# Values of a windowed attention: 128-key products against pairs of 64-key products

## The chip, the cores and the metric

The kernel is one program on one core of a Trainium2 chip, written with explicit engine queues and semaphores. The metric is the device time of one launch in microseconds (us), the median of several runs. All data on the path looked at here are float32, and each float32 matmul leaves two records on TensorE (two weight loads and two passes).

## The reference

Two stacks follow each other over 16 sequences of 256 tokens with 128 features. First one causal attention with 16 heads of 8. Then six layers, each a windowed attention with 16 heads of 64 and a gated feed-forward part. The windowed attention is where the change lies:

```python
bk2, bv2 = (look(bk), look(bv))        # each window of 32 queries sees its own 32 keys and the 32 before
sim = jnp.einsum('bhwie,bhwje->bhwij', bq, bk2) * QK_SCALE
sim = jnp.where(mask, -jnp.finfo(sim.dtype).max, sim)
attn = jax.nn.softmax(sim, -1)
out = jnp.einsum('bhwij,bhwje->bhwie', attn, bv2)
...
x = attn_layer(shift_tokens(x), Wqkv[i], q_scale[i], k_scale[i], Wo[i]) + x
x = ffn_layer(shift_tokens(x), ln_g[i], ln_b[i], W1[i], b1[i], W2[i], b2[i]) + x
```

The last product, probabilities by values, is the one that is rearranged.

## The kernel before

All activations stay on the chip. The six layers run as a pipeline over sequences: `step(n, ...)` does the projections of sequence n (head), the scores and softmax of n-1 (mid) and the output and feed-forward part of n-2 (ffn), 96 sequence-layers in all. In the middle of a layer a hardware loop runs two steps a pass, six passes; the four steps around the change of layer are written out. Each engine has its own order of work, written out by hand in its `step`, and the engines are tied by counting semaphores: `need(engine, semaphore, value)` is a wait (L40), `need_apart` a wait followed by an increment of a semaphore of its own (L47).

A sequence has two tiles (t = 0, 1) of 128 tokens, and a tile four windows of 32. For a tile, `scores` (L1389) fills two PSUM banks, SC[:, 0] and SC[:, 1] (g = 0, 1), in which ScalarE's `put_mask` (L665) has put the mask before. VectorE takes the row maximum (`row_max` L901, `less_max` L906), ScalarE the exponential (`exps` L603), VectorE the sum (L913, L916), GpSimd divides (`normalise` L462), and VectorE turns 32x32 blocks (`turn` L923) into PTr. SyncE's `band` (L309, L311) then copies the blocks by DMA into BD, a banded matrix of 128 keys by 4 windows by 16 heads by 32 queries. Its other entries are zero, cleared once.

`values(n, t, g, par)` multiplies on TensorE, for each of eight heads, the 128 keys' values (128x64 weights) by 128 columns of BD (L1344). Even and odd heads go to partitions 0 to 63 and 64 to 127 of one bank. Of tile 1's first window, the keys of the window before lie in tile 0. They come as a second product (L1349) for four heads at once: `edge_values` gathers the last 32 rows of tile 0's values into Vx, and `band` (L315) the blocks into the block-diagonal BB. ScalarE's `o_evac` (L672) copies a bank to oT, and `output` (L1356) multiplies by Wo.

The same two banks SC serve scores and values in turn: `values` of tile 0 waits until VectorE has read tile 1's scores (s_sub), and the mask for the next sequence's tile 0 goes into a bank once `o_evac` has read tile 1's values from it. The order on TensorE around the change is:

- end of a step: `hidden` 0 and 1 (L1295, feed-forward, two PSUM banks in turn), `project_q` (L1302), `values(n-1, 0, 0)`, `hidden` 2, `values(n-1, 0, 1)`, `project_k` (L1302), `feed_out` (L1399);
- next step: `turn_x` (L1279), `turn_k` (L1370), `output` (L1356), `turn_k`, `project_q`, `turn_q` (L1379), `values(n-2, 1, 0)`, `turn_q`, `values(n-2, 1, 1)`, `scores(n-1, 0, 0)`, `output`, `scores(n-1, 0, 1)`.

`hidden` 2 reuses the bank of `hidden` 0 and waits for VectorE's `gated` 0 (L929), which waits for ScalarE's `gelus` (L609). `turn_k` waits for VectorE's `over_norms` (L987). ScalarE's order behind `values(n-2, 1, .)` is o_evac of bank 0, put_mask of bank 0, o_evac of bank 1, q_evac (L654), put_mask of bank 1.

Of the kernel before, what the change touches and what calls it, by code (L numbers as in the profile page):

```python
# [12 lines left out]
P = 128  # L13
# [3 lines left out]
TILES = SEQ // P  # L17
HA, DA = 16, 8
DEPTH, HEADS, DH = 6, 16, 64
# [30 lines left out]
def build(nc, x_in, wq_t, wk_t, wv_t, wo_t, wqkv, q_scale, k_scale, wo2, ln_g, ln_b, w1, b1, w2, b2,  # L50
          c_ident, c_winmask, c_causal, c_headmask, c_rot, out):
    with ExitStack() as ctx:
# [3 lines left out]
        def sem(name):  # L56
# [45 lines left out]
        BD = sb("BD", [P, TILES, NWIN, HEADS, WIN])  # L102
        BB = sb("BB", [P, 2, 4, 2, WIN])
        Vx = sb("Vx", [P, 2, 2, P])
# [37 lines left out]
        names = ("d_x d_x2 d_wa d_wap d_rot d_c d_wq d_wk d_wv d_qks d_wo d_ln d_ff d_out i_const i_zero i_pad i_dve i_pool i_sp i_guess i_bits d_id d_wav d_hm "  # L142
# [5 lines left out]
                 "s_tab s_ct s_nq s_nk d_bd0 d_bd1 d_vx")  # L148
        S = {n: sem(n) for n in names.split()}
        (d_x, d_x2, d_wa, d_wap, d_rot, d_c, d_wq, d_wk, d_wv, d_qks, d_wo, d_ln, d_ff, d_out, i_const, i_zero, i_pad, i_dve, i_pool, i_sp, i_guess, i_bits, d_id, d_wav, d_hm,  # L150
# [5 lines left out]
         s_tab, s_ct, s_nq, s_nk, d_bd0, d_bd1, d_vx) = [S[n] for n in names.split()]  # L156
# [13 lines left out]
        N_BAND = (2 * NWIN - 1, 2 * NWIN - 1 + 4)  # L170
        N_VX = 4
# [84 lines left out]
        def _(sp):  # L256
# [46 lines left out]
            def band(n, t):  # L303

                need_apart(sp, i_sp, s_T, 2 * n + t + 1)
                need_apart(sp, i_sp, s_o, 4 * n + 2 * t - 2)
                for w in range(NWIN):
                    rows = slice(32 * w, 32 * w + 32)
                    sp.dma_start(BD[rows, t, w, :, :], PTr[t][rows, 1, :, :]).then_inc(d_bd[t], 16)  # L309
                    if w:  # L310
                        sp.dma_start(BD[32 * w - 32:32 * w, t, w, :, :], PTr[t][rows, 0, :, :]).then_inc(d_bd[t], 16)  # L311
                if t:
                    edge = PTr[t][0:WIN, 0, :, :].rearrange("p (g c k) i -> p g c (k i)", g=2, c=4)
                    for c in range(4):
                        sp.dma_start(BB[32 * c:32 * c + 32, :, c, :, :].rearrange("p g k i -> p g (k i)"),  # L315
                                     edge[:, :, c, :]).then_inc(d_bd[t], 16)

            def edge_values(n, par):

                need_apart(sp, i_sp, s_ve, 2 * n + 1)  # L320
                need_apart(sp, i_sp, s_o, 4 * n - 4)
                last = V[par][P - WIN:P, 0, :].rearrange("p (g c n) -> p g c n", g=2, c=4)
# [1226 lines left out]
```

## Time and profile before

| | |
|---|---|
| median of 3 runs | 3595.3 us (3594.93 to 3595.39) |
| profiled execution, span | 3598.4 us |
| TensorE busy | 3482.8 us, 97% |
| VectorE busy | 3160.0 us, 88% |
| ScalarE busy | 3061.0 us, 85% |
| GpSimd busy | 2352.0 us, 65% |
| chain that ended last | TensorE 62%, ScalarE 19%, issue 10%, VectorE 5% |

The span is from the first to the last instruction of one execution under the profiler, and is what that execution took. The runs without a profile lie 3 us lower. Busy time counts an engine's own instructions. A pass on TensorE is recorded with a latency that overlaps the next passes, so its pace is read from starts, or from the chain, and not from the length of one record.

### The profile page before, as it was taken

What the parts mean: (1) busy time and instruction counts of PE and PEld (TensorE: products, weight loads), DVE (VectorE), ACT (ScalarE), POOL (GpSimd) and SP (SyncE); (2) the same over time, 40 slices, a digit from 0 to 9 for tenths busy, and PEclk for the clock granted to TensorE, in tenths of its full rate; (3) what the DMA queues carried; (4) which work ended last, traced back from release to release, by engine and by line L of the source; (5) the groups of instructions that cost most, each with busy time, mean ns of one, the idle gap of its engine ahead of it and who ended that gap; (6) DMA issues with size and microseconds to landing.
All of it is one profiled execution on the core that took longest, in us unless ns stands there. A gap on an engine that the chain in (4) does not pass through costs nothing.

```text
span 3598.4 us, 95666 instructions
## 1 busy us (share of the span) xinstructions
PE 3482.8 (97%) x33868; PEld 2390.4 (66%) x33868; DVE 3160.0 (88%) x5848; ACT 3061.0 (85%) x5121; POOL 2352.0 (65%) x1607
## 2 busy tenths in 40 slices
PE   8999899999999999999999999999999999999998
PEld 6777466666666666666666666666666666666666
DVE  6998889888988988888888898888889888888986
ACT  5766688888888888888888888888888888888886
POOL 2001677777777777777777677777777777777774
PEclk9999999999999999999999999999999999999999
DMA  2000011112211112211112111112111112211112
GB/s 63 0 0 0 21 34 39 38 33 54 52 34 34 39 36 52 50 40 33 34 40 53 46 39 38 32 36 58 47 33 39 38 33 55 52 33 34 39 37 54
DMA packets 182965, 136.67 MB, mean 38 GB/s; under 512 B 97612, under 2 KB 135632, under 8 KB 182800
## 3 DMA queue, kind: packets, MB, share of 16 engines
q1 hardware_dynamic: 180019, 125.00, 14.8%
q10 hardware_dynamic: 2781, 9.51, 0.9%
q8 instruction: 98, 1.61, 0.2%
q14 instruction: 67, 0.55, 0.1%
HBM read 19.04 MB, written 2.10 MB: 6 GB/s over the span
## 4 chain that ended last, share of the span: by engine, by line
PE 62%; ACT 19%; issue 10%; DVE 5%; SPq 1%; POOL 1%; DMA 1%; ACTq 0%; DVEq 0%; POOLq 0%
PE ps L1302 12%; PE ps L1389 10%; PE ps L1356 10%; PE ps L1344 7%; PE ps L1379 4%; PE ps L1370 4%; PE ps L1160 3%; ACT L750 3%; ACT area L603 2%; DVE area L987 2%; ACT G L609 2%; ACT L609 2%; ACT area L618 2%; ACT area L625 2%; PE ps L1295 2%
## 5 line engine op out<-in xcount | busy, mean ns | idle before, releaser
L1302 PE MATMUL ps<-Wqkv,xsT 128*128 128x512 f32 x2304 | 1112.5, 605 | 8.7 <-ACT area L638 3.8
L449 POOL TENSOR_TENSOR area<-area,tab 128x512 f32<-128x512 f32 x768 | 970.0, 1273 | 146.7 <-ACT area L618 146.1
L1302 PEld LDWEIGHTS ps<-Wqkv,xsT 128*128 128x128 f32 x2304 | 391.2, 189 | 351.4 <-issue 295.0
L462 POOL TENSOR_TENSOR area<-area,lsum 128x1024 f32<-128x1024 f32 x192 | 365.5, 1904 | 383.2 <-DVE lsum L916 383.2
L456 POOL TENSOR_TENSOR AQb<-AQb,area 128x1024 f32<-128x1024 f32 x192 | 455.2, 2371 | 15.1
L456 POOL TENSOR_TENSOR area<-area 128x1024 f32<-128x1024 f32 x192 | 455.0, 2370 | 9.0 <-DVE area L976 1.5
L618 ACT ACTIVATE area<-ps 128x1024 f32<-128x1024 f32 x384 | 393.6, 1025 | 66.2 <-PE ps L1302 55.1
L1389 PEld LDWEIGHTS ps<-kbd,area 128*32 128x32 f32 x12288 | 313.2, 109 | 196.1 <-issue 113.4
L1344 PE MATMUL ps<-BD,area 128*64 128x128 f32 x6144 | 421.5, 279 | 17.7 <-issue 11.3
L1344 PEld LDWEIGHTS ps<-BD,area 128*64 128x64 f32 x6144 | 329.4, 137 | 158.8 <-issue 100.2
L1389 PE MATMUL ps<-kbd,area 128*32 128x128 f32 x12288 | 415.6, 276 | 17.0 <-ACT kbd L648 5.7
L625 ACT ACTIVATE area<-area 128x1024 f32<-128x1024 f32 x384 | 405.1, 1055 | 3.2
L1356 PE MATMUL ps<-Wo,area 128*128 128x128 f32 x3072 | 385.2, 279 | 1.2 <-ACT area L672 0.7
L1356 PEld LDWEIGHTS ps<-Wo,area 128*128 128x128 f32 x3072 | 357.6, 192 | 20.7 <-issue 19.6
L654 ACT ACTIVATE area<-ps 128x512 f32<-128x512 f32 x384 | 217.9, 593 | 132.6 <-PE ps L1379 132.6
L901 DVE TENSOR_REDUCE mx<-ps 128x8 f32<-128x512 f32 x384 | 263.2, 686 | 49.7 <-PE ps L1389 49.7
L923 DVE STREAM_TRANSPOSE area<-area 128x1024 f32<-128x1024 f32 x192 | 239.2, 1246 | 61.7 <-POOL area L462 61.2
L1295 PE MATMUL ps<-xnT,W 128*128 128x256 f32 (+1 forms) x1152 | 288.3, 386 | 1.8 <-ACT xnT L684 1.5
L672 ACT ACTIVATE area<-ps 128x512 f32<-128x512 f32 x384 | 227.0, 591 | 71.0 <-PE ps L1349 66.8
L906 DVE TENSOR_TENSOR area<-ps,mx 128x512 f32<-128x512 f32 x384 | 264.8, 690 | 9.9
L1295 PEld LDWEIGHTS ps<-xnT,W 128*128 128x128 f32 (+1 forms) x1152 | 197.8, 178 | 91.3 <-issue 63.6
L941 DVE TENSOR_REDUCE ss<-area 128x16 f32<-128x1024 f32 x192 | 233.6, 1216 | 22.4 <-ACT area L625 21.2
(136 smaller groups left out, 6630.6 us busy)
## 6 DMA issues: line engine op xcount, KB each, us to landing
BD<-area SPq DMA_DIRECT2D x1344, 64.0 KB, 2.0
Vx<-area SPq DMA_DIRECT2D x384, 32.0 KB, 1.9
Wqkv<-ffn_Wqkv ACTq DMA_DIRECT2D x18, 512.0 KB, 4.0
BB<-area SPq DMA_DIRECT2D x384, 16.0 KB, 1.8
x2s<-x2s SPq DMA_DIRECT2D x96, 56.0 KB, 2.0
Wo<-ffn_Wo SPq DMA_DIRECT2D x6, 512.0 KB, 4.3
W<-ffn_W SPq DMA_DIRECT2D x6, 341.0 KB
x2s<-x2s SPq DMA_DIRECT2D x96, 0.2 KB, 1.7
```

The source lines that it names most:

```text
L449: pool.tensor_tensor(b4[:, :, here], q4[:, :, there], s4[:, :, here], ALU.mult).then_inc((s_bq, s_bk)[j], 1)
L456: pool.tensor_tensor(AQ[t][:, col], AQ[t][:, col], BQ[:, col], ALU.add).then_inc(s_rot, 1)
L462: pool.tensor_tensor(p3, p3, lsum[:, 1, :].unsqueeze(2).broadcast_to([P, HEADS, 2 * WIN]), ALU.mult).then_inc(s_pn, 1)
L618: act.activation(QH[:, j * INNER:(j + 1) * INNER], PJ[:, :], ACT.Copy).then_inc((s_hq, s_hk)[j], 1)
L625: act.activation(SQ[:, col], QH[:, col], ACT.Square).then_inc((s_sqq, s_sqk)[j], 1)
L901: dve.tensor_reduce(mx[:, 8 * g:8 * g + 8], s3[:, g, :, :], AX.X, ALU.max).then_inc(s_mx, 1)
L906: dve.tensor_tensor(Pr[:, t, 512 * g:512 * g + 512].rearrange("p (h k) -> p h k", k=2 * WIN), s3[:, g, :, :], mx[:, 8 * g:8 * g + 8].unsqu ...
L1295: last = mm(TR[c % 2][0:m, half * SEQ:(half + 1) * SEQ], W1[:, half * FF + f0:half * FF + f0 + m], xnT[:, :], start=True, stop=True)
L1302: last = mm(PJ[:, b * 512:(b + 1) * 512], xsT[:, par, t * P:(t + 1) * P], Wqkv[:, w0:w0 + 512], start=True, stop=True)
L1344: last = mm(slot[DH * k:DH * k + DH, c * P:(c + 1) * P], V[par][:, t, h * DH:(h + 1) * DH], BD[:, t, :, h, :], start=(c == 0), stop=False, ...
L1356: last = mm(EXO[:, t * P:(t + 1) * P], oT[:, t, c, :], Wo[:, c, :], start=(c == 0), stop=(c == PAIRS - 1))
L1389: last = mm(SC[32 * w:32 * w + 32, g, (c % 4) * P:(c % 4 + 1) * P], qT[:, c, 32 * w:32 * w + 32], kbd[:, c, :, k0:k0 + 2 * WIN], start=Fal ...
```

## The change

The 128 keys of a tile are taken as two halves r of 64. Each half multiplies only its own 64 queries (two windows, 64 columns), uses its own 64 rows of the array and writes its own PSUM bank: bank r now holds the queries of half r for all 16 heads, where bank g held all queries for eight heads. For a head there are two products of 64 keys by 64 value columns by 64 queries instead of one of 128 by 64 by 128. BD shrinks to half.

What crosses a half is done afterwards as products over 32 rows. The keys of window 1 for the queries of window 2 are 16 products in either tile. Tile 0's last 32 keys for tile 1's first window are 16 more in tile 1. Their blocks are in the new BE. Vx, BB and `edge_values` (eight DMAs a sequence) go away, and one DMA into BE is added. `values` does a whole tile in one call, with one increment of s_o, and stands once where it stood twice: for tile 1 before the second `turn_q`, for tile 0 after `hidden` 2. Its three waits are `need_apart`.

```diff
-        BD = sb("BD", [P, TILES, NWIN, HEADS, WIN])
-        BB = sb("BB", [P, 2, 4, 2, WIN])
-        Vx = sb("Vx", [P, 2, 2, P])
+        BD = sb("BD", [P, TILES, 2, HEADS, WIN])
+        BE = sb("BE", [P, TILES, HEADS, WIN])
...
-        N_BAND = (2 * NWIN - 1, 2 * NWIN - 1 + 4)
-        N_VX = 4
+        N_BAND = (2 * NWIN - 1, 2 * NWIN)
...
                 need_apart(sp, i_sp, s_T, 2 * n + t + 1)
-                need_apart(sp, i_sp, s_o, 4 * n + 2 * t - 2)
+                need_apart(sp, i_sp, s_o, 2 * n + t - 1)
+                rows = [slice(32 * w, 32 * w + 32) for w in range(NWIN)]
                 for w in range(NWIN):
-                    rows = slice(32 * w, 32 * w + 32)
-                    sp.dma_start(BD[rows, t, w, :, :], PTr[t][rows, 1, :, :]).then_inc(d_bd[t], 16)
-                    if w:
-                        sp.dma_start(BD[32 * w - 32:32 * w, t, w, :, :], PTr[t][rows, 0, :, :]).then_inc(d_bd[t], 16)
-                if t:
-                    edge = PTr[t][0:WIN, 0, :, :].rearrange("p (g c k) i -> p g c (k i)", g=2, c=4)
-                    for c in range(4):
-                        sp.dma_start(BB[32 * c:32 * c + 32, :, c, :, :].rearrange("p g k i -> p g (k i)"),
-                                     edge[:, :, c, :]).then_inc(d_bd[t], 16)
-
-            def edge_values(n, par):
-
-                need_apart(sp, i_sp, s_ve, 2 * n + 1)
-                need_apart(sp, i_sp, s_o, 4 * n - 4)
-                last = V[par][P - WIN:P, 0, :].rearrange("p (g c n) -> p g c n", g=2, c=4)
-                for c in range(4):
-                    sp.dma_start(Vx[32 * c:32 * c + 32, par, :, :], last[:, :, c, :]).then_inc(d_vx, 16)
+                    sp.dma_start(BD[rows[w], t, w % 2, :, :], PTr[t][rows[w], 1, :, :]).then_inc(d_bd[t], 16)
+                    if w % 2:
+                        sp.dma_start(BD[rows[w - 1], t, 1, :, :], PTr[t][rows[w], 0, :, :]).then_inc(d_bd[t], 16)
+                    elif w or t:
+                        sp.dma_start(BE[rows[w - 1], t, :, :], PTr[t][rows[w], 0, :, :]).then_inc(d_bd[t], 16)
 
             def shift(n, last):
...
-                    edge_values(n - 1, 1 - par)
...
-            pool.memset(BB[:, :, :, :, :], 0.0).then_inc(i_zero, 1)
...
-                need(act, s_o, 4 * n - 4)
+                need(act, s_o, 2 * n - 2)
...
             def o_evac(n, t, g):
-                need(act, s_o, 4 * n + 2 * t + g + 1)
+                need(act, s_o, 2 * n + t + 1)
                 if t == 0 and g == 0:
                     need(act, s_wo, n)
-                act.activation(oT[:, t, 4 * g:4 * g + 4, :], SC[:, g, :].rearrange("p (c n) -> p c n", c=4),
+                half = slice(2 * WIN * g, 2 * WIN * (g + 1))
+                act.activation(oT[:, t, :, half], SC[:, g, :].rearrange("p (c n) -> p c n", c=PAIRS),
                                ACT.Copy).then_inc(s_oe, 1)
...
-            def values(n, t, g, par):
-
-                T = 2 * n + t
-                if g == 0:
-                    need(pe, s_ve, T + 1)
+            def values(n, t, par):
+
+                need_apart(pe, i_pe, s_ve, 2 * n + t + 1)
+                need_apart(pe, i_pe, d_bd[t], 16 * N_BAND[t] * (n + 1))
+                if t:
+                    need_apart(pe, i_pe, s_oe, 4 * n + 2)
+                else:
+                    need_apart(pe, i_pe, s_sub, 4 * n + 4)
+                for c in range(PAIRS):
+                    for r in range(2):
+                        keys = slice(2 * WIN * r, 2 * WIN * (r + 1))
+                        for k in range(2):
+                            h = 2 * c + k
+                            mm(SC[DH * k:DH * k + DH, r, 2 * WIN * c:2 * WIN * (c + 1)], V[par][keys, t, h * DH:(h + 1) * DH],
+                               BD[keys, t, :, h, :], start=(c == 0), stop=False, skip_group_check=True)
+                for c in range(PAIRS):
+                    for k in range(2):
+                        h = 2 * c + k
+                        last = mm(SC[DH * k:DH * k + DH, 1, 2 * WIN * c:2 * WIN * c + WIN], V[par][WIN:2 * WIN, t, h * DH:(h + 1) * DH],
+                                  BE[WIN:2 * WIN, t, h, :], start=False, stop=True, skip_group_check=True)
                     if t:
-                        need(pe, d_vx, 16 * N_VX * (n + 1))
-                    need(pe, d_bd[t], 16 * N_BAND[t] * (n + 1))
-                if t:
-                    need(pe, s_oe, 4 * n + g + 1)
-                else:
-                    need(pe, s_sub, 4 * n + 3 + g)
-                slot = SC[:, g, :]
-                for c in range(4):
-                    for k in range(2):
-                        h = 2 * (4 * g + c) + k
-                        last = mm(slot[DH * k:DH * k + DH, c * P:(c + 1) * P], V[par][:, t, h * DH:(h + 1) * DH],
-                                  BD[:, t, :, h, :], start=(c == 0), stop=False, skip_group_check=True)
-                if t:
-                    for k in range(2):
-                        half = slice(DH * k, DH * k + DH)
-                        last = mm(slot[half, :].rearrange("p (c n) -> p c n", c=4)[:, :, 0:WIN], Vx[:, par, g, half],
-                                  BB[:, g, :, k, :], start=False, stop=True, skip_group_check=True)
+                        for k in range(2):
+                            h = 2 * c + k
+                            last = mm(SC[DH * k:DH * k + DH, 0, 2 * WIN * c:2 * WIN * c + WIN], V[par][P - WIN:P, 0, h * DH:(h + 1) * DH],
+                                      BE[P - WIN:P, t, h, :], start=False, stop=True, skip_group_check=True)
                 last.then_inc(s_o, 1)
...
                 if ffn:
-                    values(n - 2, 1, 0, par)
+                    values(n - 2, 1, par)
                 if mid:
                     turn_q(n - 1, 0, 1)
-                if ffn:
-                    values(n - 2, 1, 1, par)
                 if mid:
                     scores(n - 1, 0, 0)
                 if ffn:
@@ -1477,12 +1463,10 @@
                     hidden(n - 2, 1)
                 if head:
                     project_q(n, 1, par)
-                if mid:
-                    values(n - 1, 0, 0, 1 - par)
                 if ffn:
                     hidden(n - 2, 2)
                 if mid:
-                    values(n - 1, 0, 1, 1 - par)
+                    values(n - 1, 0, 1 - par)
                 if head:
                     project_k(n, 1, par)
                 if ffn:
```

## Rows read from the trace of the kernel before

**Rows 1.** The page, section 1: busy us (share of the span), instructions of each engine.

```profile
PE 3482.8 (97%) x33868; PEld 2390.4 (66%) x33868; DVE 3160.0 (88%) x5848; ACT 3061.0 (85%) x5121; POOL 2352.0 (65%) x1607
```

**Rows 2.** Windows, two loop steps: length, busy us (instructions) of each engine, granted clock, DMA.

```profile
2178.00:2244.10 66.10, 64.76 (x634) 44.20 (x632) 59.11 (x107) 58.57 (x93) 47.66 (x33) 1.00 0.16 36
```

**Rows 3.** TensorE in order of time, one loop step: start, length in us, group [idle before].

```profile
2207.90 1.09 PE L1344 MATMUL ps<-BD,area 128*64 128x128 f32 x16
...
2208.93 1.10 PE L1295 MATMUL ps<-xnT,W 128*85 128x256 f32 x4
...
2210.97 1.98 PE L1302 MATMUL ps<-Wqkv,xsT 128*128 128x512 f32 x4
...
2214.13 0.38 PE L1279 MATMUL ps<-ident,xst 128*128 128x128 f32 x2
...
2214.69 0.66 PE L1370 MATMUL ps<-ident,area 128*128 128x128 f32 x4 [0.17 <-DVE area L987]
...
2219.68 1.09 PE L1344 MATMUL ps<-BD,area 128*64 128x128 f32 x16
...
2220.61 0.39 PE L1349 MATMUL ps<-BB,Vx 128*64 128x128 f32 x4
...
2222.76 1.08 PE L1389 MATMUL ps<-kbd,area 128*32 128x128 f32 x32
```

**Rows 4.** VectorE and ScalarE in order of time, the same step.

```profile
2193.83 0.69 DVE L901 TENSOR_REDUCE mx<-ps 128x8 f32<-128x512 f32 x1 [0.47 <-PE ps L1389]
...
2208.16 0.47 DVE L929 SCALAR_TENSOR_TENSOR H<-ps,b1s,G 128x256 f32<-128x256 f32 x1
...
2213.41 1.22 DVE L987 TENSOR_TENSOR area<-area,ps 128x1024 f32<-128x1024 f32 x1
...
2221.05 0.60 ACT L672 ACTIVATE area<-ps 128x512 f32<-128x512 f32 x1
...
2221.68 0.60 ACT L665 ACTIVATE ps<-wmask_f 128x512 f32<-128x512 f32 x1
```

**Rows 5.** Chain in order of time: start, us, line, passes.

```profile
2217.60 1.72 PE ps L1302 x4
...
2219.32 0.44 PE ps L1379 x4
...
2221.59 1.02 PE ps L1344 x16
...
2222.83 1.01 PE ps L1389 x32
```

**Rows 6.** TensorE in windows of 0.03 and 0.05 us: passes that run in them.

```profile
2222.76 0.32 PE L1389 MATMUL ps<-kbd,area 128*32 128x128 f32 x4
...
215.27 0.38 PE L1149 MATMUL ps<-area,AqT 32*128 32x128 f32 x2
```

**Rows 7.** Groups of weight loads by form: busy us, mean ns, idle before.

```profile
L1344 PEld LDWEIGHTS ps<-BD,area 128*64 128x64 f32 x6144 | 329.4, 137 | 158.8 <-issue 100.2 <-DMA BD<-area 56.7 <-DMA BB<-area 2.0
...
L1389 PEld LDWEIGHTS ps<-kbd,area 128*32 128x32 f32 x12288 | 313.2, 109 | 196.1 <-issue 113.4 <-ACT kbd L648 69.0 <-ACT ps L665 2.3
```

**Rows 8.** Waiting and register operations of the queues (L40), 2222.2 to 2223.2.

```profile
L40 PEldq ALU_OP  x2: 32/32/32, 2222.3 to 2223.0; - x2
```

**Rows 9.** GpSimd's increment (L47) between 2207 and 2210, and GpSimd in order of time.

```profile
L47 POOLq EVENT_SEMAPHORE  x1: 17/17/17, 2208.4 to 2208.4; - x1
...
2207.24 1.91 POOL L462 TENSOR_TENSOR area<-area,lsum 128x1024 f32<-128x1024 f32 x1 [1.09 <-DVE lsum L916]
```

**Rows 10.** DMA issues: SyncE's queue in order of time; the page, section 6.

```profile
2215.09 2.56 SPq L315 DMA_DIRECT2D BB<-area  x4
...
BB<-area SPq DMA_DIRECT2D x384, 16.0 KB, 1.8
```

**Rows 11.** DMA queue of instructions, 1915 to 2113 and 2113 to 2434: packets, MB, share.

```profile
q8 instruction: 13, 0.21, 0.5%
...
q8 instruction: 1, 0.02, 0.0%
```

More of the change, by code:

```diff
@@ L139, in build @@
         nmx = sb("nmx", [P, 2, HA])
-        names = ("d_x d_x2 d_wa d_wap d_rot d_c d_wq d_wk d_wv d_qks d_wo d_ln d_ff d_out i_const i_zero i_pad i_dve i_pool i_sp i_guess i_bits d_id d_wav d_hm "
+        names = ("d_x d_x2 d_wa d_wap d_rot d_c d_wq d_wk d_wv d_qks d_wo d_ln d_ff d_out i_const i_zero i_pad i_dve i_pool i_sp i_guess i_bits i_pe d_id d_wav d_hm "
                  "a_lnc a_lnr a_lnn a_xh a_xt a_xe a_qk a_qe a_ke a_km a_v a_ve a_s a_mx a_e a_t a_te "
@@ L147, in build @@
                  "s_o s_oe s_ve s_wo s_r1 d_sh s_lnc s_lnr s_lnn s_ln s_xn s_xne s_h s_gl s_g s_y s_xc "
-                 "s_tab s_ct s_nq s_nk d_bd0 d_bd1 d_vx")
+                 "s_tab s_ct s_nq s_nk d_bd0 d_bd1")
         S = {n: sem(n) for n in names.split()}
-        (d_x, d_x2, d_wa, d_wap, d_rot, d_c, d_wq, d_wk, d_wv, d_qks, d_wo, d_ln, d_ff, d_out, i_const, i_zero, i_pad, i_dve, i_pool, i_sp, i_guess, i_bits, d_id, d_wav, d_hm,
+        (d_x, d_x2, d_wa, d_wap, d_rot, d_c, d_wq, d_wk, d_wv, d_qks, d_wo, d_ln, d_ff, d_out, i_const, i_zero, i_pad, i_dve, i_pool, i_sp, i_guess, i_bits, i_pe, d_id, d_wav, d_hm,
          a_lnc, a_lnr, a_lnn, a_xh, a_xt, a_xe, a_qk, a_qe, a_ke, a_km, a_v, a_ve, a_s, a_mx, a_e, a_t, a_te,
@@ L155, in build @@
          s_o, s_oe, s_ve, s_wo, s_r1, d_sh, s_lnc, s_lnr, s_lnn, s_ln, s_xn, s_xne, s_h, s_gl, s_g, s_y, s_xc,
-         s_tab, s_ct, s_nq, s_nk, d_bd0, d_bd1, d_vx) = [S[n] for n in names.split()]
+         s_tab, s_ct, s_nq, s_nk, d_bd0, d_bd1) = [S[n] for n in names.split()]
         PJ = ps[:, 0:2, :].rearrange("p a b -> p (a b)")
@@ L373, in _ @@
             pool.memset(x2s[:, :, :, :], 0.0).then_inc(i_zero, 1)
-            pool.memset(BB[:, :, :, :, :], 0.0).then_inc(i_zero, 1)
             pool.wait_ge(d_hm, 16)
-            pool.wait_ge(i_zero, 5)
+            pool.wait_ge(i_zero, 4)
             pool.wait_ge(i_pad, 2)
@@ L589, in _ @@
             attention_steps(act, a_step)
-            act.wait_ge(i_zero, 7)
+            act.wait_ge(i_zero, 6)
             def x_evac(n, par):
```

## The prediction, made before the kernel was run

> **What bounds the kernel now.** I read the page's first section, then the windows, then one step in order of time, engine by engine, and last the chain. TensorE is busy for 97% of the span [rows 1], and at full clock in the middle of a layer: of the 66.10 us of one pass of the loop (two steps) it is busy for 64.76, VectorE for 59.11, ScalarE for 58.57 [rows 2]. So a step lasts 33.05 us, and whatever lengthens or shortens TensorE's own sequence moves the end, unless TensorE then only waits. The 97% hides how near some waits are: in the order of time TensorE's value groups (L1344, L1349) fill stretches in which the other engines are just getting ready [rows 3, 4]. These decide the case.
>
> How fast the small products go: a pass is one of the two records that each float32 matmul leaves. Four passes over 512 columns take 1.72 us, 0.43 each; four over 128 columns take 0.44, 0.11 each; so a pass costs its moving columns at 0.84 ns [rows 5]. The 16 value passes take 1.02 us and the 32 score passes 1.01 [rows 5]: 128 columns each, two and four side by side, eight groups of 0.11 plus 0.15 for changing shape. The 256-column group of L1295 says the same: 4 x 0.216 = 0.86, and 1.02 from its start to the next [rows 3]. Passes of different column tiles start together (four L1389 in a window of 0.03 us), and so do two that use different 32-row tiles (L1149) [rows 6]. Weight loads are recorded with 109 ns for 32 columns and 137 for 64 [rows 7]: 0.88 ns a column, so some 56 ns for 64 columns apart from a fixed delay that overlaps.
>
> **The change, part by part**, in one loop step.
>
> *Main products.* 32 passes of 128 columns for each tile t become 64 passes of 64 columns, four side by side. 64 columns stream in 0.054 us, their 64 weights load in 0.056: I take 0.057 for each group of four, 16 groups, 0.91 us. Before: 16 pairs at 0.11, 1.75 us.
>
> *Crossing blocks.* Tile 0 had none; tile 1 had eight passes, 0.44 us. Now tile 0 has 32 passes and tile 1 has 64, each with 32 moving but still 64 weight columns. By streaming a group would cost 0.027, by its weights 0.056; a weight load can hide only behind a pass as long as itself, so I take 0.057, and both tiles need 16 groups (pairs for tile 0, fours for tile 1): 0.91 us. With two changes of shape (128 to 64 rows, then 32 rows), 0.30, a block lasts 2.12 us. The lower bound (0.028) is 1.66 us.
>
> *Tile 0's place.* Before, half of its values (2207.90) stood between project_q and hidden(2) (2208.93) [rows 3]. Without it hidden(2) reaches TensorE at once, but needs VectorE's gated(0), which ends at 2208.16 + 0.47 = 2208.63; it would start at 2208.70 (L1370 started 0.06 after its L987). VectorE is no help: from the row maximum at 2193.83, which itself waited for TensorE, to gated(0) it has 27 rows with three pauses, 0.5 us in all [rows 4]. So TensorE stands idle for 0.9 us that was filled. Then hidden(2) 1.02, block 2.12: project_k at 2211.84 instead of 2210.97, +0.87. Later turn_k waits for L987 (ends 2214.63): TensorE could have been there at 2214.13 + 0.22 = 2214.35 but started at 2214.69 [rows 3, 4]; 0.34 of the delay vanishes in this wait. Net +0.53.
>
> *Tile 1's place.* Before: values, crossing, turn_q, values, crossing, 2219.68 to 2222.76, 3.08 us [rows 3]. Behind the first half ScalarE read bank 0 (L672 at 2221.05) and wrote the mask there (L665, ends 2222.28) while TensorE did the other half [rows 4]; the scores of bank 0 need that mask. In the new order both banks finish together, and only turn_q (0.59) covers the two. The first half's last product began at 2220.72, the mask was usable at 2222.28 + 0.06: 1.62 us. The new block's last product begins 1.97 after 2219.68, at 2221.65, so the scores start at 2223.27 instead of 2222.76: +0.51. ScalarE's next work (second bank, q_evac, mask of bank 1) is queued behind its wait, but the scores of bank 0 (1.01) and the output products behind them cover it.
>
> *Issue.* Tile 1's block is 256 instructions in 1.97 us, tile 0's 192. The queue's own records show how fast they can be sent: between two register operations of TensorE's sequencer, at 2222.3 and 2223.0, lie the 64 instructions of one score group, 11 ns each [rows 8]. 256 would need 2.8 us; those sent ahead during the transposes come off. From none ahead (+0.85) to all ahead (0) I take +0.15, since the sequencer no longer waits there for the last band transfer. That makes tile 1 +0.66.
>
> *TensorE's own increments* (three per block): on GpSimd such an increment ran at 2208.4, in the middle of L462 (2207.24 to 2209.15) and ahead of L456, which stands before it in GpSimd's order [rows 9], so it does not drain an engine; I take nothing. If it drained TensorE, blocks would lose what was sent ahead: up to +1.
>
> *Transfers.* Four BB and four Vx transfers go, one BE comes. BB's were the last to land for tile 1: issued 2215.09 to 2217.65, 1.8 us to landing [rows 10], 0.2 us before the values at 2219.68. That wait was hidden; its margin grows to some 2 us, worth nothing by itself. ScalarE's reads have new strides and the same size: nothing. GpSimd clears less memory in the first part, off the chain.
>
> Sum: 0.53 + 0.66 = 1.19 us a step, 96 steps, 114 us; on the profiled span 3598.4 + 114 = 3712, and on the median of the runs, which is 3.1 us under that span, 3709.
>
> The Trainium skill (TensorE: Matmul & The Clock Gate, "Wait — 56ns, not 53.3ns?") says that starts of matmuls are never closer than about 25 ns. By that rule the 128 passes of tile 1 would need 3.2 us and the 96 of tile 0 2.4, about 1.8 us a step more than my sum, and the kernel would take near 3880. By that rule, the trace disagrees: it has four starts inside 0.03 us [rows 6].
>
> **Rivals.**
> *Row halves in turn.* Passes in the same columns but different rows do not overlap once 64-wide. For it: no row shows four tiles in both directions. Against it: L1149. Main groups then cost 0.11 and tile 1's crossing too: +0.9 for tile 0, +1.8 for tile 1, 3.9 us a step, 3970.
> *An issue limit.* The fastest pace of the chain is 32 passes in 1.01 us, 0.0315 each [rows 5]. If that were sending and not streaming, 128 passes would take 4.0 us and 96 take 3.0: +3.2 us, 4.4 a step, 4020. Against it: the 11 ns above.
> *The loop's code no longer stays in place.* In a layer's unrolled steps and first loop pass instruction transfers run (13 in 198 us); in the other five passes one in 321 us [rows 11]. A pass has 634 matmul and 633 weight-load records, plus some 50 others [rows 2]; 608 are added, 45% more. If that is too long, each jump back waits for a transfer: 0.5% of 16 engines over 198 us for 13 is 1.2 us each, and about 2 to land, as the band's; partly covered by queued passes. 30 jumps at 1 to 3 us: +30 to +90 on top of my sum, 3740 to 3800.
> The Trainium skill (Runtime: NRT & Kernel Launch, "Instruction fetch mechanics") gives TensorE 2048 instructions in blocks of 256 and a stall for a jump out of them; the new pass has near 1,930, so close that its position among the blocks would decide. That the present loop is not fetched again agrees with the rows.
> *Crossing passes that cost only their issue* (the other side). If weights of 32-row tiles load while other rows' tiles run, they shrink towards 7 ns, and the block to 1.3 us. Tile 0: 2211.02, lost in the wait of L1370; tile 1: scores at 2222.55, -0.2. 3575. It decides once a block is under 1.6 us, below my bound by streaming; L1344 and L1389 show no pass below its columns.
> *Streaming bound only* (0.028): blocks of 1.66 us, +0.07 and +0.05 to +0.3, 3605 to 3630.
>
> **Numbers.** Forecast 0.62 (own range 3670 to 3765), loop code 0.14, row halves 0.07, issue limit 0.05, streaming bound 0.06, issue-only crossings 0.06. A difference of 0.2% (7 us) is what can be told from none. Faster 0.06, same 0.03, slower 0.91. The range 3620 to 3870 leaves out row halves, the issue limit, issue-only crossings and a little of streaming, some 0.19 in all.
>
> **What would show it.** After: L1344's groups of 64 in about 1 us with four starts together; the crossing lines in about 0.9 us each; TensorE idle near 0.9 us before L1295's 85-column group, released by VectorE's H; idle near 0.9 us before the scores, released by ScalarE's L665 mask; less wait at L1370 for L987. It is wrong if blocks are not near 2.1 us (weights or issue), if either wait is missing, or if instruction transfers go on through the loop.

## The result and the profile after

The changed kernel takes 3775.2 us (median of 4 runs, 3774.2 to 3782.0) against 3595.4 (3594.9 to 3596.6) in the same session: 1.050 times as long, 95% interval 1.0487 to 1.0517. The forecast was 3709. It names the right sign and, as will be seen, some two thirds of the loss (114 of 180 us); the rest is what the rival on the loop's code describes. The measured time lies above the forecast's own range (3670 to 3765), inside that rival's (3740 to 3800) and inside the wide range (3620 to 3870). Each group of runs below was taken beside runs of the kernel before, whose median lay between 3595 and 3598 from group to group, so a few us between groups mean nothing. One of the ten executions of e2_before_no_loop took 4921.3 us at a granted clock of 0.655 and is left out of its ratio.

The page of the changed kernel: busy us and instructions of each engine, from section 1, and the queue of instructions from section 3 (packets, MB, share of 16 engines).

```profile
span 3772.4 us, 124129 instructions
...
PE 3480.3 (92%) x48460; PEld 2424.7 (64%) x48460; DVE 3176.6 (84%) x5848; ACT 3057.5 (81%) x5121; POOL 2346.6 (62%) x1606
...
q8 instruction: 427, 7.00, 0.8%
```

TensorE has 14,592 more passes than in [rows 1], and yet is busy for 2.5 us less; its share fell from 97% to 92%. So the span's 174 us are idle time of TensorE. The waits name it. Before, TensorE's longest ones were (line that waits, what released it, us in total, times, longest):

```profile
PE ps L1370 <- ACT area L654: 33.4, 96, 1.2
PE ps L1370 <- DVE area L987: 15.2, 72, 1.4
PE ps L1344 <- issue: 11.3, 11, 2.3
```

After, in the same view (L1377 are the scores, L1281 `hidden`, L1265 `turn_x`, L1358 `turn_k`, L1344 `output`):

```profile
PE ps L1377 <- ACT ps L650: 79.3, 96, 1.9
PE ps L1281 <- DVE H L915: 69.3, 96, 2.2
PE ps L1265 <- issue: 43.8, 30, 2.2
PE ps L1358 <- ACT area L639: 33.2, 96, 1.0
...
PE ps L1344 <- issue: 6.7, 6, 1.3
```

Three new waits: the scores for ScalarE's mask and hidden 2 for VectorE's H, both 96 times, and `turn_x` for nothing that the profile shows, 30 times. The wait for VectorE's norms (old L987) is nearly gone (2.3 us, twice). 79.3 + 69.3 + 43.8 - 15.2 is 177 us, the 174 within what smaller waits add and take. The queue of instructions from 2113 to 2434 us, where [rows 11] have a single packet:

```profile
q8 instruction: 40, 0.66, 0.9%
```

So instruction transfers now go on through the loop, which the prediction had named as a sign of being wrong. One step in order of time on TensorE, after (L1288 projections, L1327 main products, L1332 crossing, L1387 `feed_out`, L1367 `turn_q`):

```profile
2229.41 1.09 PE L1281 MATMUL ps<-xnT,W 128*85 128x256 f32 x4 [0.71 <-DVE H L915]
2230.43 1.16 PE L1327 MATMUL ps<-BD,area 64*64 64x64 f32 x64
2231.52 1.12 PE L1332 MATMUL ps<-BE,area 32*64 32x32 f32 x32
2232.57 1.98 PE L1288 MATMUL ps<-Wqkv,xsT 128*128 128x512 f32 x4
2234.39 1.50 PE L1387 MATMUL ps<-W,H 128*128 128x128 f32 x12
2237.41 0.43 PE L1265 MATMUL ps<-ident,xst 128*128 128x128 f32 x2 [1.52 <-issue]
2237.68 0.60 PE L1358 MATMUL ps<-ident,area 128*128 128x128 f32 x4
...
2242.59 1.16 PE L1327 MATMUL ps<-BD,area 64*64 64x64 f32 x64
...
2244.74 0.66 PE L1367 MATMUL ps<-ident,area 128*128 128x128 f32 x4
...
2246.24 1.08 PE L1377 MATMUL ps<-kbd,area 128*32 128x128 f32 x32 [0.84 <-ACT ps L650]
```

Read from start to start: the main products of tile 0 take 1.09 us and its crossing 1.05, the block 2.14; tile 1's block 2.15, with 256 instructions. The row of L1265 is the surprise: `feed_out` ends near 2235.9, and `turn_x`, which was to follow at once as in [rows 3], comes 1.5 us later. It stands at the head of a loop pass. Steps from one `turn_x` to the next that hold no such stall last 34.08 us at least and often 34.17 (before: 33.05); those that end in one last 35.3 to 36.8, one of them 37.7.

### The profile page after: what moved, and what is told of

Its sections match the earlier page's. It is cut to its first block, busy times and chain, and to the rows that moved or that the text cites. A ratio compares the mean times of both kernels' runs of the same rounds, so it can differ in the third digit from the quotient of the medians.

```text
span 3772.4 us, 124129 instructions
## 1 busy us (share of the span) xinstructions
PE 3480.3 (92%) x48460; PEld 2424.7 (64%) x48460; DVE 3176.6 (84%) x5848; ACT 3057.5 (81%) x5121; POOL 2346.6 (62%) x1606
## 4 chain that ended last, share of the span: by engine, by line
PE 66%; DVE 11%; ACT 11%; issue 8%; DMA 2%; SPq 1%; POOL 1%; DVEq 0%; ACTq 0%; POOLq 0%
PE ps L1288 13%; PE ps L1344 10%; PE ps L1377 9%; PE ps L1327 6%; PE ps L1332 5%; PE ps L1387 3%; PE ps L1358 3%; PE ps L1281 3%; DVE ss L927 3%; PE ps L1146 3%; DVE lsum L899 3%; ACT area L610 3%; DVE area L962 2%; PE ps L1367 2%; DMA x2s<-x2s 2%
## 5 line engine op out<-in xcount | busy, mean ns | idle before, releaser
L1288 PE MATMUL ps<-Wqkv,xsT 128*128 128x512 f32 x2304 | 1112.6, 605 | 9.0 <-ACT area L623 3.8
L1288 PEld LDWEIGHTS ps<-Wqkv,xsT 128*128 128x128 f32 x2304 | 391.3, 189 | 339.3 <-issue 278.8
L1377 PE MATMUL ps<-kbd,area 128*32 128x128 f32 x12288 | 419.6, 277 | 97.4 <-ACT ps L650 79.3
L1377 PEld LDWEIGHTS ps<-kbd,area 128*32 128x32 f32 x12288 | 316.4, 110 | 284.6 <-issue 178.1
L1344 PE MATMUL ps<-Wo,area 128*128 128x128 f32 x3072 | 394.7, 282 | 8.1 <-issue 6.7
L1344 PEld LDWEIGHTS ps<-Wo,area 128*128 128x128 f32 x3072 | 361.5, 193 | 35.8 <-issue 27.9
L1281 PE MATMUL ps<-xnT,W 128*128 128x256 f32 (+1 forms) x1152 | 287.0, 385 | 70.8 <-DVE H L915 69.3
L1281 PEld LDWEIGHTS ps<-xnT,W 128*128 128x128 f32 (+1 forms) x1152 | 197.0, 178 | 221.6 <-DVE H L915 147.9
L962 DVE TENSOR_TENSOR area<-area,ps 128x1024 f32<-128x1024 f32 x192 | 228.7, 1191 | 76.4 <-PE ps L1367 75.6
L650 ACT ACTIVATE ps<-wmask_f 128x512 f32<-128x512 f32 x384 | 229.3, 597 | 64.0 <-DVE area L892 60.9
L420 POOL COPY xres<-x2s 128x256 f32 (+1 forms) x80 | 31.8, 397 | 383.7 <-DVE x2s L987 383.7
```

Source lines behind the costliest of these rows:

```text
L962: dve.tensor_tensor(AQ[t][:, col].rearrange("p (h d) -> p h d", d=DH), QH[:, col].rearrange("p (h d) -> p h d", d=DH), cosp[:, t, j, :].un ...
L1281: last = mm(TR[c % 2][0:m, half * SEQ:(half + 1) * SEQ], W1[:, half * FF + f0:half * FF + f0 + m], xnT[:, :], start=True, stop=True)
L1288: last = mm(PJ[:, b * 512:(b + 1) * 512], xsT[:, par, t * P:(t + 1) * P], Wqkv[:, w0:w0 + 512], start=True, stop=True)
L1344: last = mm(EXO[:, t * P:(t + 1) * P], oT[:, t, c, :], Wo[:, c, :], start=(c == 0), stop=(c == PAIRS - 1))
L1377: last = mm(SC[32 * w:32 * w + 32, g, (c % 4) * P:(c % 4 + 1) * P], qT[:, c, 32 * w:32 * w + 32], kbd[:, c, :, k0:k0 + 2 * WIN], start=Fal ...
```

## The experiments

Twelve kernels. The first four ask where the time at the head of the loop comes from, the next two what a crossing product costs, the last six what the two waits are worth. A ratio is against the kernel before, with its 95% interval. Where TensorE's steps are "written out", its twelve middle steps of a layer stand in the program one after the other, without the hardware loop; the other engines keep their loops.

**e1_no_loop: the change, TensorE's steps written out.**

```diff
-            stack_steps(pe, step)
+            stack_steps(pe, step, looped=False)
```

> The changed kernel with TensorE's program written out in full (no hardware loop on TensorE; the other engines keep theirs, the order of work is the same). Theory: the waits and the longer order cost about 1.1 us a step (a step without a jump lasts 34.1 us instead of 33.05), and the rest of the +180 us is a stall of TensorE at the jump back, since a pass of the loop no longer stays in its instruction memory. Then this kernel takes 3775 - 70 = 3705 us (3695 to 3715), every step lasts about 34.1 us, and the instruction transfers stay near 400. Rival: what costs is the transfer of the code itself, or the sending of more instructions, everywhere: then the time stays at 3765 to 3780.

Measured 3713.5 us, 1.0319 (1.0301 to 1.0336). Waits of TensorE, written out:

```profile
PE ps L1381 <- ACT ps L654: 74.0, 96, 1.9
PE ps L1285 <- DVE H L919: 69.6, 96, 2.2
PE ps L1362 <- ACT area L643: 39.8, 96, 1.1
```

`turn_x` no longer waits; the mask and H waits stand as they were. Nearly as many instruction packets come as in the changed kernel (364 against 427), and nearly all of them are hidden here (ten waits inside the crossing products, 5.4 us together, are not): 62 us go with the jumps, 2.1 for each of 30. Without them the kernel takes close to what was forecast for it (3709).

**e2_before_no_loop: the kernel before, written out the same way.** 

> The kernel before with TensorE's program written out in full. Theory of the jumps: the loop of before fits, so it pays no stall and there is nothing to gain but what registers cost; the written-out steps of before last 32.8 to 33.0 us against 33.05 in the loop, so 3575 to 3596 us, although instruction transfers rise from 98 to about 270. Rival (transfers themselves cost TensorE time): 170 more transfers make it slower, by 0.4 us each at the rate of the changed kernel (70 us for its 330 more... some 0.2 each), 3625 to 3660.

Measured 3604.0, 1.0017 (1.0007 to 1.0027), inside neither range: writing out gives nothing back, nor does it cost 30 us. TensorE waits 18.4 us at the values (26 times) for nothing that the profile shows, where before had 11.3 (11 times); only one of the 26 has an instruction packet shortly ahead of it, so this is not shown to be late code. So the 62 us are the changed kernel's own. Set like against like, both written out, the change costs 3713.5 - 3604.0 = 109.5 us, and the other 70 of the 180 come only with the loop.

**e7_no_crossing: the change without its crossing products,** in the loop. What crosses a half is left out of the output. A pass of the loop loses 384 instructions, of some 1,930.

```diff
-                               BD[keys, t, :, h, :], start=(c == 0), stop=False, skip_group_check=True)
-                for c in range(PAIRS):
...
+                               BD[keys, t, :, h, :], start=(c == 0), stop=True, skip_group_check=True)
```

> The changed kernel without its crossing products (L1332, L1337), so their part of the output is left out. A pass of TensorE's loop then has some 1,550 instructions instead of 1,930 (before: 1,310). Theory: it fits again, so instruction transfers fall from 427 to near 110, and no pass of the loop has the idle 1.5 us before turn_x; with 1.1 us less in each block the time is 3520 to 3560 us. Rival (it is not the length but any growth of the loop): transfers stay above 300 and every second step is longer by over 1 us: 3590 to 3630.

Measured 3533.7 (one run). Nearly every step in the loop lasts 32.55 to 32.65 us and TensorE is never idle ahead of `turn_x` there. Its queue of instructions:

```profile
q8 instruction: 115, 1.88, 0.2%
```

With about 1,550 instructions in a pass (1,930 less 384) the stall is absent; but this kernel also does less work, so the next one changes the length alone.

**e12_before_four_steps: the kernel before, four steps in a pass** (three passes a layer, some 2,630 instructions each), same order and work.

```diff
-                with eng.Fori(0, SEQS // 2 - 2) as k:
-                    for odd in range(2):
-                        step(eng.snap(base + 2 * k + (2 + odd)), 2 * k + (2 + odd), odd, True, True, True, layer)
+                with eng.Fori(0, (SEQS - 4) // each) as k:
+                    for i in range(each):
+                        step(eng.snap(base + each * k + (2 + i)), each * k + (2 + i), i % 2, True, True, True, layer)
```

> The kernel before with four steps to a pass of TensorE's loop instead of two (three passes a layer instead of six); the work and its order are the same. Its pass has some 2,620 instructions. Theory (length alone makes the stall): it no longer fits, instruction transfers rise from 98 to about 250, and each of the 12 jumps back costs 1.5 to 2.5 us: 3595 + 18 to 30 = 3613 to 3625 us. Rival (the stall needs the dense blocks of the changed kernel): 3590 to 3602.

Measured 3650.3, 1.0152 (1.0139 to 1.0166), 53 us over the kernel before in the same session: the direction expected, about twice the size. Its waits:

```profile
PE ps L1279 <- issue: 22.6, 12, 2.3
PE ps L1344 <- DMA BD<-area: 10.8, 19, 1.1
...
PE ps L1344 <- issue: 9.6, 8, 2.3
...
PE ps L1356 <- issue: 6.5, 4, 2.1
```

Two jumps back in each of six layers, 12 in all, and 12 stalls of 1.9 us ahead of `turn_x` (old L1279), where before's list of waits has none. So the length of a pass makes the stall, in the kernel before too. The stalls are 22.6 of 53 us. Four more just behind a jump (L1356, 6.5 us) follow an instruction packet in the same way (see e11 for that reading). Most of the rest is a longer wait for the band (10.8 us against 1.8) and 9.7 us more of busy TensorE; the eight waits at the values (L1344, 9.6 us) follow no packet and were there before.

**e4_half_weights and e8_eight_columns: what bounds a crossing product.** e4 takes 32 of a head's 64 value columns in the crossing products, e8 takes 8 of their 32 moving columns; the other half, and the other three quarters, of the crossing output are left out. For e4 (the products into bank 0 likewise)

```diff
-                        last = mm(SC[DH * k:DH * k + DH, 1, 2 * WIN * c:2 * WIN * c + WIN], V[par][WIN:2 * WIN, t, h * DH:(h + 1) * DH],
+                        last = mm(SC[DH * k:DH * k + WIN, 1, 2 * WIN * c:2 * WIN * c + WIN], V[par][WIN:2 * WIN, t, h * DH:h * DH + WIN],
```

and for e8

```diff
-                        last = mm(SC[DH * k:DH * k + DH, 1, 2 * WIN * c:2 * WIN * c + WIN], V[par][WIN:2 * WIN, t, h * DH:(h + 1) * DH],
-                                  BE[WIN:2 * WIN, t, h, :], start=False, stop=True, skip_group_check=True)
+                        last = mm(SC[DH * k:DH * k + DH, 1, 2 * WIN * c:2 * WIN * c + 8], V[par][WIN:2 * WIN, t, h * DH:(h + 1) * DH],
+                                  BE[WIN:2 * WIN, t, h, 0:8], start=False, stop=True, skip_group_check=True)
```

> The changed kernel with the crossing products (L1332, L1337) on only the first 32 of the 64 value columns of each head, so half of their output is left out; their number and their 32 moving columns stay. Theory: a group of crossing passes is bound by loading 64 weight columns (0.057 us); with 32 it takes 0.03, so tile 0's crossing falls from 1.05 us to about 0.6 and the block from 2.14 to 1.7 us. Rival: each pass is bound by its sending or by a fixed floor: the crossing stays at 1.05 us.

> The changed kernel with 8 moving columns instead of 32 in each crossing product, so three quarters of the crossing output are left out; weights as they were. Theory (bound by 64 weight columns): tile 0's crossing stays at 1.05 us and the time at 3765 to 3780. Rival (bound by streaming): it falls to 0.4 us or less and the time to under 3700.

Measured 3726.8 and 3772.3 (one run each; the changed kernel 3775.2). TensorE in order of time at tile 0, e4:

```profile
2242.95 1.16 PE L1327 MATMUL ps<-BD,area 64*64 64x64 f32 x64
2244.04 0.69 PE L1332 MATMUL ps<-BE,area 32*32 32x32 f32 x32
2244.67 1.98 PE L1288 MATMUL ps<-Wqkv,xsT 128*128 128x512 f32 x4
```

The same place, e8:

```profile
2232.44 1.16 PE L1327 MATMUL ps<-BD,area 64*64 64x64 f32 x64
2233.53 1.10 PE L1332 MATMUL ps<-BE,area 32*64 32x8 f32 x32
2234.56 0.70 PE L1288 MATMUL ps<-Wqkv,xsT 128*128 128x512 f32 x1
```

Half the weight columns: 1.05 us become 0.63. A quarter of the moving columns: 1.03, no change. Each of the 16 groups of a tile's crossing products costs what 64 weight columns cost, 0.06 us, though it streams only 32. Whether that is the load itself or something else that goes with the 64 columns, such as the 64 output rows, these two runs do not separate.

**e10_split_no_loop: the H wait filled again.** Tile 0's main products (part 0 of `values`) go back ahead of hidden 2, its crossing (part 1) stays behind; written out, so to be set against e1.

```diff
                     project_q(n, 1, par)
+                if mid:
+                    values(n - 1, 0, 1 - par, 0)
                 if ffn:
                     hidden(n - 2, 2)
                 if mid:
-                    values(n - 1, 0, 1 - par)
+                    values(n - 1, 0, 1 - par, 1)
```

> e5's split of tile 0's block with TensorE's program written out, so without jumps. Theory: the wait for VectorE's H costs 0.35 us a step net of one change of shape and of the slack before turn_k: 3713 - 34 = 3679 us (3670 to 3690). Rival (the split has no gain, what e5 gained was noise of the jumps): 3705 to 3715.

Measured 3668.5, 1.0195 (1.0179 to 1.0211), 45 us under e1 and 11 under the 3679 expected. The H wait (69.6) is gone; it is worth 45 and not 70, because 26.8 us come back as a wait of L1332, here the main products, for the band's transfers, in 32 of 96 steps. It has the lowest median of the changed versions that compute everything (e9's runs overlap it) and is still 71 us slower than the kernel before in the same session.

**e5_split_tile0: the same in the loop.** 

> The changed kernel with tile 0's block cut in two: the main products ahead of hidden 2, the crossing products behind it. e3 showed that the whole block ahead only moves the wait (TensorE then stood before turn_k for over_norms, because hidden 2 and the third gelu came 1.2 us later). Theory: as in the kernel before, about 1.1 us ahead of hidden 2 covers the wait for VectorE's H without making hidden 2 late; against the changed kernel project_k comes 0.65 us earlier (0.8 of wait less 0.15 for one more change of shape), 0.3 of it is lost before turn_k: -0.35 us a step, 3740 us (3725 to 3755), with the idle time before the 85-column L1281 and before turn_k both under 15 us. Rival: any order but the one of before loses the same: 3765 to 3830.

Measured 3763.6, 1.0464 (1.0446 to 1.0483): only 12 us under the changed kernel and 24 over what was expected, where e10 gained 45 on e1. The steps that begin behind a stall and meet nothing else do shorten, from 34.2 to 33.4 us, by more than the 0.35 expected. But the band is waited for as in e10 (23.9 us, 28 times), the stalls at the jump grew from 43.8 to 57.3 us, and behind some of them TensorE is slow. TensorE in order of time, e5:

```profile
2221.23 0.49 PE L1265 MATMUL ps<-ident,xst 128*128 128x128 f32 x2 [2.01 <-issue]
...
2222.37 3.15 PE L1347 MATMUL ps<-Wo,area 128*128 128x128 f32 x16
```

Windows of the same stretch, e5 (length, busy us of PE, PEld, DVE, ACT, POOL, granted TensorE clock, DMA share, GB/s):

```profile
2220.00:2222.00 2.00, 0.77 (x5) 0.78 (x6) 2.00 (x3) 0.52 (x2) 1.92 (x3) 0.87 0.36 80
2222.00:2226.00 4.00, 4.00 (x24) 3.99 (x23) 2.59 (x6) 1.80 (x5) 3.92 (x3) 0.64 0.07 14
2226.00:2230.00 4.00, 4.00 (x132) 2.77 (x130) 1.82 (x4) 3.24 (x6) 1.61 (x1) 1.00 0.00 0
```

The output group (L1347) takes 3.15 us where it takes 1.95 at full clock. The clock fell to its half level, 1.2 GHz (0.50 granted from 2221.5 to 2224.8), after 2.0 us of idle time. That happened behind 11 of the 30 stalls of this run; others of the same length left the clock at 1.00. Over the whole execution the mean granted clock is 0.990 where the changed kernel has 0.997, and TensorE is busy for 3499 us instead of 3480 with the same passes.

**e3_tile0_first: all of tile 0's block ahead of hidden 2.** 

> The changed kernel with tile 0's block of values ahead of the third chunk of the feed-forward (hidden 2) instead of behind it. Theory: in the changed kernel TensorE waits there 0.8 to 0.9 us for VectorE's H; the block (2.14 us) covers it, project_k comes 0.85 us earlier, of which 0.3 is lost again in the wait for over_norms: -0.5 us a step, 3775 - 48 = 3727 us (3710 to 3745). The idle time before L1281 falls from 69 us to under 5. Rival: VectorE moves with TensorE, so that the wait comes back elsewhere: 3765 to 3780.

Measured 3832.7, 1.0661 (1.0643 to 1.0678): 106 us over what was expected, and over the rival's range too. The H wait goes, and a bigger one comes, with longer stalls at the jump and a wait for the band. Waits of e3:

```profile
PE ps L1358 <- DVE area L973: 81.1, 66, 1.4
...
PE ps L1265 <- issue: 65.6, 30, 2.6
...
PE ps L1327 <- DMA BD<-area: 23.8, 27, 3.2
```

A block of 2.1 us ahead of hidden 2 fills 0.9 us of idle and delays hidden 2 by 1.2. ScalarE in order of time, e3, shows what hangs on it:

```profile
2230.50 0.47 ACT L594 ACTIVATE G<-ps,b1s 85x256 f32<-85x256 f32 x1 [0.92 <-PE ps L1281]
2230.98 1.28 ACT L736 ACT_TABLE_LOAD   x1
2232.28 0.23 ACT L615 ACTIVATE ss<-ss 128x32 f32<-128x32 f32 x1
2232.54 0.32 ACT L617 ACTIVATE ss<-ss,consts 128x32 f32<-128x32 f32 x1
```

The third `gelus` waits 0.92 for TensorE, and a table load and the norms' ss stand behind it; VectorE idles 1.26 for that ss, its L973 starts at 2233.76, and `turn_k` needs L973: 1.2 us in each of 66 steps. The expectation counted TensorE's time alone and not what hangs on hidden 2; its rival had VectorE late, but as much only as the H wait had been. Against the changed kernel, -69 (H) + 79 (L973) + 22 (jumps) + 24 (band) is 56 us of a span that grew by 57.

**e11_early_no_loop: the mask wait filled.** `project_q(n, 0)` (1.7 us) now stands between the second turn_q and the scores that wait, because turn_q and the values go ahead of it; ScalarE's `keep_raw` and VectorE's `cosines` of it move behind the masks and the row maximum (not printed). Written out, against e1.

```diff
+                if mid:
+                    turn_q(n - 1, 0, 0)
...
+                if ffn:
+                    values(n - 2, 1, par)
+                if mid:
+                    turn_q(n - 1, 0, 1)
                 if head:
...
                     project_q(n, 0, par)
...
                 if mid:
-                    turn_q(n - 1, 0, 0)
...
-                if ffn:
-                    values(n - 2, 1, par)
-                if mid:
-                    turn_q(n - 1, 0, 1)
...
                     scores(n - 1, 0, 0)
```

> e6's place of project_q with TensorE's program written out. Theory: the wait of the scores for the mask costs 0.8 us a step: 3713 - 79 = 3634 us (3625 to 3645). What kept e6 at 3768 with the loop were stalls of TensorE in the steps behind a jump back (idle 28 us before L1331, released by nothing that the profile shows), from code that came late, and not ScalarE or VectorE. Rival (the move makes another engine late in every second step): 3680 or more.

Measured 3719.7, 1.0335 (1.0319 to 1.0351): no gain at all on e1, 86 us over what was expected. The number falls in the rival's range (3680 or more), but no new wait for ScalarE or VectorE explains it. Its waits:

```profile
PE ps L1284 <- DVE H L918: 70.3, 96, 2.2
...
PE ps L1335 <- issue: 19.4, 14, 2.0
PE ps L1340 <- issue: 17.9, 13, 1.8
```

The mask wait (74 us) is gone and ordinary steps fell by 0.5 us, from 34.17 to 33.67. But inside the crossing products (L1335, L1340) TensorE now stands idle 27 times for 1.4 us, released by nothing that the profile shows, in a program without jumps; in order of time such a row reads:

```profile
2495.75 0.24 PE L1335 MATMUL ps<-BE,area 32*64 32x32 f32 x2 [1.62 <-issue]
```

That returns 37 us. The trace shows what these 27 idle times have in common. A packet of the queue of instructions (16 KB, on average one in 10 us) starts 2.2 to 2.8 us before TensorE goes on, and its transfer ends 1.2 to 1.6 us before, all 27 times. The same holds for the stalls ahead of `turn_x`: in all 30 of the changed kernel and all 12 of e12 the last packet ended 1.4 to 1.7 us before TensorE went on. For the idle times that e2 has at the values it holds once in 26. So TensorE stands in e11 for code that comes late, in a program without jumps. Why the packet comes late here and seldom in e1 is not shown.

The mean clock fell from 0.996 to 0.991 and TensorE's busy time rose by 31 us, from 3471.0 to 3501.8. The sum, -74 + 37 + 31, is -6 for the three; the profiled span rose by 11, so smaller waits took some 17 more.

**e6_early_tile1: the same in the loop.** 

> The changed kernel with project_q(n, 0) (1.7 us on TensorE) put between turn_q(0, 1) and scores(0, 0), so that it covers ScalarE's read of bank 0 and the mask; ScalarE's copy of it and VectorE's cosines(n, 0, 0) move behind the masks and behind less_max(0, 0). Nothing is added or removed. Theory: the idle time of TensorE before the scores (79 us, released by the mask) goes: -0.8 us a step, 3775 - 78 = 3697 us (3685 to 3715). Rival: ScalarE or VectorE then become late for scores(0, 1), the sum of squares or the rotation, and the wait comes back there: 3740 to 3800.

Measured 3768.2, 1.0491 (1.0466 to 1.0515): 7 us under the changed kernel, with overlapping runs, so no difference that can be told, and 71 us over what was expected. The written-out steps around a change of layer last 33.63 at least, 0.45 less than in the changed kernel. In the loop, steps that begin behind a stall last 33.25 at least, 0.9 less; those that end in one take 34.8 to 38.5. The stalls at `turn_x` are 40.2 us, and TensorE stands again inside the crossing products (28.0 us, 22 times), each time behind an instruction packet as in e11.

**e9_both_no_loop: the edits of e10 and e11 together.** 

> The changed kernel with both moves (e5's split of tile 0's block and e6's place of project_q) and TensorE's program written out (e1). With the loop, e6's ordinary steps fell from 34.1 to 33.25 us and e5's to 33.75, but the steps after a jump back grew. Theory: written out, the gains add: 3713 - 96 x (0.83 + 0.35) = 3600 us (3590 to 3615), a step of 32.9 to 33.0 us, about the kernel before and not better, since two blocks of 2.14 us and the added changes of shape cost what the packed products of before cost. Rival: one move uses up the slack of the other (ScalarE or VectorE late): 3630 to 3680.

Measured 3674.8, 1.0208 (1.0189 to 1.0226): 75 us over what was expected. Ordinary steps last 32.9 us, less than before's 33.05, so if all 96 were like them the change would break even. The rest is 33 us of idle within the crossing products (23 times, each behind an instruction packet as in e11), 30.9 for the band (43 times), and 38 us more of busy TensorE than in e1, at a mean clock of 0.989. The rival's range (3630 to 3680) holds the number, though what it named, ScalarE or VectorE late, is not what the waits show.

## Why the prediction was right, and by how much it fell short

**The blocks (2.12 us forecast): 2.14 and 2.15.** Four tiles do run at once: four L1327 start inside 0.03 us, and 64 passes take 1.09 us. Row halves in turn and the issue limit are out. The Trainium skill (TensorE: Matmul & The Clock Gate, "Wait — 56ns, not 53.3ns?") gives 25 ns as the least time between starts; for these passes, which lie in different tiles of the array, the trace disagrees with 17 ns each. A group's cost goes by its weight columns (e4, e8), which was the choice made; streaming alone would have given 0.028 a group.

**Tile 0's place.** From project_q to project_k 5.86 us against 4.98 before: +0.88, forecast +0.87. Project_q's row before, which with project_k at 2210.97 in [rows 3] gives the 4.98:

```profile
2205.99 1.99 PE L1302 MATMUL ps<-Wqkv,xsT 128*128 128x512 f32 x4
```

The idle time ahead of hidden 2 is released by H as named; the profile shows 0.7 us of it. The prediction says 0.9, but its own times (2207.90 and 2208.70) give 0.80, and its sum uses the times. From project_k to turn_k, where no jump lies between, 3.38 against 3.72: the 0.34 of L987's wait vanish as forecast. Net +0.54.

**Tile 1's place.** From the values to the scores 3.65 against 3.08: +0.57, forecast 0.51 for the mask and 0.15 for issue. The mask term alone is enough; the 256 instructions cost no more than their weights, so the issue term of 0.15 us a step was nothing, and so were the three increments, as far as shows.

**The sum.** 0.54 + 0.57 = 1.11 us a step, 107 us over 96, against 114 forecast; the steps at a change of layer are slower still. e1, which has these waits and no jumps, came out at 3713.5 for 3709, and against e2 the change costs 109.5 us. That this half of the argument holds is shown. That e1 agrees to 5 us is partly luck: the issue term had put 14 us into the sum that were not there, and some steps are longer than 34.17. "One BE comes" is a net count: a sequence has three transfers into BE more and two into BD fewer, which changes no term.

**The step that failed** is the sum's last line: it added nothing for instruction transfers and left the loop's code a rival at 0.14, priced at +30 to +90 on top. It measured +62 (e1), or 70 against e2, and both happened together: 3709 + 62 is 3771. It was not an alternative to the two waits but a further term. The profile had the sign of it: [rows 11] show the present loop as never fetched again, and the text itself counted 1,930 instructions for the new one. With a body 45% longer and no row for where it stops staying in place, a chance of 0.14 was low; a chance near a half would have put the time as likely near 3770 as near 3709. The runs show no stall at about 1,320 and about 1,550 instructions a pass and one at every jump back at about 1,930 and 2,630. The Trainium skill (Runtime: NRT & Kernel Launch, "Instruction fetch mechanics") gives PE room for 2048 instructions, refilled in blocks of 256, and says that a taken branch out of the current two-page window stalls. The packets here are of 16 KB, as it says, and a jump over more than it keeps does stall. But about 1,930 is under its 2048 and stalls all the same, and about 1,320 is more than two blocks and does not stall; where between 1,550 and 1,930 the limit lies, and whether the place among the blocks moves it, no run tells.

**What stays open.** Why code comes late inside the crossing products in e11, e9 and e6 and seldom in e1 and e10. They are the densest stretch of the program (256 instructions in 2.15 us), but they are so in e1 too. What the idle times of before and e2 at the values wait for. And what decides whether the clock falls behind a stall.

## What to carry to other kernels

Where an engine that is the bound gets a wait filled by small work, moving that work away costs what it covered, here 1.1 us a step, although the value products themselves became shorter, 4.3 us a step against 4.55; look first at what each group of instructions stands in front of. Count instructions as well as time: a loop body that grows by 45% can cross from "stays in place" to "fetched on every pass", here at 2 us a jump. And price a filled wait by what is late next: six kernels here removed a wait of about 70 us or more, and none gave back more than 45.

## What the hardware showed that was not expected

- A loop pass of about 1,320 or 1,550 TensorE instructions runs without a stall at its head; one of 1,930 stalls 1.46 us in the mean, 30 times of 30, and one of 2,630 stalls 1.9 us, 12 of 12. The same order as straight code runs with nearly as many instruction transfers and hardly a wait behind one (e1: 5.4 us in ten; e2: 0.2 in one). But straight code is not safe from it: moving one group of instructions brought 37 us in 27 waits (e11).
- After an idle time of 2.0 us (e5) and 2.3 us (e3) the granted clock was at its half level through most of the next output group, which took 0.9 to 1.2 us longer. It happened behind 11 of 30 stalls in either. The length of the idle time alone does not decide it: in the changed kernel one of 1.85 us (1329.2) brought the clock down, and the output group took 3.55 us, while one of 2.17 us (1890.7) left it at 1.00 and the group at 1.95. So a stall can cost more than itself, and filling one wait can lay bare this second price at another.
- Passes over 32 rows with 64 weight columns cost 0.06 us for a group of four or two tiles, with 8 moving columns as with 32 (e8); with 32 weight columns it is 0.04 (e4).
- A late instruction packet shows in the trace: its transfer ends 1.2 to 1.7 us before TensorE goes on, in every one of 30 stalls of the changed kernel, 12 of e12 and 27 of e11.
